# A two-layer pre-norm decoder on one core: norm statistics, causal maxima, rounding and residual biases moved between the engines, with new lists of the order of work

## The chip, the cores and the metric

The kernel runs on one core of a Trainium2 chip. A core has five engines with an instruction queue each, worked off in order: TensorE (PE; its weight loads are shown as PEld), VectorE (DVE), ScalarE (ACT), GpSimd (POOL) and SyncE (SP), which here only issues DMAs. They wait for one another by semaphores. Sums of products land in PSUM, everything else is in SBUF. The metric is the device time of one execution in microseconds (us); lower is better.

## What is computed

The input is 64 sequences of 128 tokens with 256 features, a context of the same shape and a mask. Six residual blocks follow one another, each on the layer norm of x, all in float32:

```python
x = x + L0_attn(layernorm(x))      # window attention: 7 neighbours, 16 heads; + bo
x = x + L0_xattn(layernorm(x))     # masked cross-attention to ctx; (.. @ Wp.T + bp) * mask
x = x + L0_ffn(layernorm(x))       # routing to 64 slots, a GRU step, back; + bo
x = x + L1_attn(layernorm(x))      # causal attention with a learned bias by position; + bproj
x = x + L1_xattn(layernorm(x))     # cross-attention to ctx; + bo
x = x + L1_ffn(layernorm(x))       # quantised linear, depthwise conv, silu, quantised linear

def layernorm(x):  m = mean(x, -1);  return (x - m) / sqrt(mean((x - m)**2, -1) + 1e-5)
# causal attention: att = softmax(q k / 4 + bias[h, t, s]), bias = -inf for s > t
# quantised linear: q = clip(round(x * s), -128, 127) / s, s = 127 / max|x| over the row
```

## The kernel before

Work comes in pieces of two sequences (B = 2). Four chains (0 to 3) take 8 turns each; a turn is all six blocks for one piece, so 32 pieces in all. A chain owns two PSUM banks, a tile `xa` (the residual stream, 128 tokens x 2 x 256), a tile `xn` (normalised x, reused in between) and an arena. The blocks are tagged a, b, f, 1, x, g in the order above.

Each engine's program of a turn is a Python generator (`vector_turn`, `scalar_turn`, `tensor_turn`, `pool_turn`, `sync_turn`), and each `yield` ends a step. `ORDER` holds for every engine a string of digits, one per step: the chain whose next step the engine's queue gets (`in_order`). So the interleaving of the chains on each engine is fixed in advance by these lists, and an engine that comes to a step whose operands are not there stands still, with everything behind it. From the third turn the strings repeat with every turn of the four chains; this text calls one repetition a round. All events of a chain are counted on one semaphore per engine, in the order that `TABLES` lists.

The parts that the change touches:

- A norm (`norm_vector`, L674 to L679): DVE takes statistics of each sequence (two `bn_stats`, two `bn_aggr`), adds 1e-5. GpSimd (`norm_pool`, L1515 to L1519) negates the mean, raises the variance to the power -0.5, multiplies both. ACT (L968) writes `xn = xa * rs + nm` for each sequence, and PE transposes it (L1170).
- Causal maxima (`maxima_vector`, L692 and L696): for each of 8 groups of four heads, DVE adds `pos_bias` to the scores in PSUM and writes them to SBUF (128x512), then reduces them to the negated maxima. ACT (L1034) takes `exp(s + m)`, one instruction per head, and PE transposes the result (L1286). The other two attentions call the same function with the reduction alone.
- Residual biases: bo, bproj and box are split into three bfloat16 parts in setup (L441 to L457); in each of the three blocks PE adds them by one product `pick` x `bias3` (L1319) in front of the projection (L1322). The addition to `xa` is one DVE instruction (L717, L792, L854), called y here.
- Rounding in g: DVE multiplies the hidden values by a scale (L904), ACT adds 12582912 (L1156), DVE subtracts it and casts to bfloat16 (L908).

Of the kernel before, what the change touches and what calls it, by code (L numbers as in the profile page):

```python
# [38 lines left out]
class Events:  # L39
# [10 lines left out]
    def now(self, name):  # L50
# [14 lines left out]
        wd_zero ones no_bias rel pos_max wd0 wd1 wd2 wd3 c2 bvw0 bvw1 bw10 bw11 bwx0 bwx1 slots c4 c5 c6 w1t_abs
        w1t_mean w1t_rec w1t_round w1t_min w1t c8 c9 c10 c_cw pos_eps pos_rec rel_norm c11 w2t_abs w2t_mean w2t_rec
        w2t_round w2t_min w2t c13 c14 c15 conn_d slot_mean slotT fire_b0 fire_b1 fire_b2 fire_b3 gate_b half_hn wvo
        bvo bias1 biasx bias_r0 bias_p0 bias_s0 bias_r1 bias_p1 bias_s1 bias_r2 bias_p2 bias_m0 bias_m1 bias_m2
# [4 lines left out]
        b_ve b_mx0 b_mx1 b_mx2 b_mx3 b_mx4 b_mx5 b_mx6 b_mx7 b_rc b_rm b_o b_y f_st0 f_st1 f_mv0 f_mv1 f_ve f_l
        f_top0 f_top1 f_sub f_mr0 f_mr1 f_m f_em f_s f_r f_al f_w1 f_w2 f_ac f_rz f_n1 f_n2 f_n3 f_u1 f_u2 f_u3 f_sv
        f_y 1_st0 1_st1 1_mv0 1_mv1 1_ve 1_bi0 1_mx0 1_bi1 1_mx1 1_bi2 1_mx2 1_bi3 1_mx3 1_bi4 1_mx4 1_bi5 1_mx5
        1_bi6 1_mx6 1_bi7 1_mx7 1_rc 1_o 1_y x_st0 x_st1 x_mv0 x_mv1 x_ve x_mx0 x_mx1 x_mx2 x_mx3 x_mx4 x_mx5 x_mx6
        x_mx7 x_rc x_o x_y g_st0 g_st1 g_mv0 g_mv1 g_ve g_am g_cl g_rc g_bk g_sc g_q2 g_hp0 g_hp1 g_t00 g_t01 g_t20
# [1728 lines left out]
```

## Time and profile before

| | |
|---|---|
| three runs | 3289.53, 3285.29, 3288.36 us; median 3288.36 |
| the profiled execution | 3283.83 us, its span 3282.0 us, mean granted clock 0.955 |
| PE, busy | 2836.4 us, 86% of the span |
| DVE, busy | 2522.0 us, 77% |
| ACT, busy | 2178.7 us, 66% |
| POOL, busy | 755.3 us, 23% |
| chain that ended last | PE 49%, DVE 31%, ACT 11%, POOL 4%, issue 4%, DMA 1% |

The spread of the three runs is 4 us. A busy share is an average over the whole span; which engine the others wait for changes inside a round, so the stretches have to be looked at apart. Instructions of one engine overlap a little: the busy time of a group is less than its count times the mean duration of one.

### The profile page before, as it was taken

The numbers are of one execution on the slowest core, as the hardware profiler recorded it, in microseconds if no ns is written. First come the engines' busy times: TensorE is split into PE (matmuls) and PEld (weight loads), VectorE is DVE, ScalarE is ACT, GpSimd is POOL, SyncE is SP. The second block draws the span as 40 slices with busy tenths as digits, with TensorE's granted clock in tenths as the row PEclk, the third lists the DMA queues.
The fourth block names the chain that finished last, engine by engine and source line by source line (L and its number), as shares of the span: only waits on it lengthen the run. The fifth ranks groups of instructions, "written<-read, shape, count | busy, mean of one in ns | idle before, by whom it ended". The sixth has DMA issues, their size and how long they took to land.

```text
span 3282.0 us, 59801 instructions
## 1 busy us (share of the span) xinstructions
PE 2836.4 (86%) x23406; PEld 2073.9 (63%) x23406; DVE 2522.0 (77%) x5446; ACT 2178.7 (66%) x4271; POOL 755.3 (23%) x1360
## 2 busy tenths in 40 slices
PE   3799986999878998899988998889988999889985
PEld 3566754676656766577666676567665676656763
DVE  6856599766898579975898769986799768987676
ACT  2368764678646876577855777657865687557773
POOL 1420013300233112330133112422032301232100
PEclk8799997999989999899999999999999999999996
DMA  5000010000000000000000000000000000000000
GB/s 157 1 1 1 4 27 17 1 1 5 24 12 9 1 16 12 20 1 1 16 21 11 1 4 13 24 9 1 5 24 12 9 1 16 16 17 1 1 1 13
DMA packets 43468, 43.47 MB, mean 13 GB/s; under 512 B 8577, under 2 KB 41185, under 8 KB 43185
## 3 DMA queue, kind: packets, MB, share of 16 engines
q1 hardware_dynamic: 41200, 36.46, 3.8%
q8 instruction: 184, 3.01, 0.4%
q10 hardware_dynamic: 1984, 3.18, 0.3%
q14 instruction: 100, 0.81, 0.1%
HBM read 31.24 MB, written 8.39 MB: 12 GB/s over the span
## 4 chain that ended last, share of the span: by engine, by line
PE 49%; DVE 31%; ACT 11%; POOL 4%; issue 4%; DMA 1%; SPq 0%; DVEq 0%; POOLq 0%; ACTq 0%
PE banks L1179 8%; PE banks L1213 7%; DVE chain_m L696 5%; PE banks L1322 4%; PE banks L1222 4%; PE banks L1260 4%; PE banks L1197 3%; DVE chain_arena L890 3%; PE banks L1286 2%; DVE chain_arena L927 2%; PE banks L1406 2%; DVE chain_arena L730 2%; DVE chain_arena L931 2%; DVE chain_stat L674 2%; DVE chain_arena L774 2%
## 5 line engine op out<-in xcount | busy, mean ns | idle before, releaser
L1213 PE MATMUL banks<-chain_arena 64*128 64x256 f32 x3072 | 426.2, 399 | 42.4 <-DVE chain_m L696 28.1
L696 DVE TENSOR_REDUCE chain_m<-banks 128x4 f32<-128x512 f32 x512 | 328.7, 681 | 84.8 <-PE banks L1213 84.2
L1515 POOL TENSOR_SCALAR chain_ng<-chain_sv 128x2 f32<-128x2 f32 x192 | 52.9, 276 | 1408.4 <-DVE chain_sv L677 1408.3
L1213 PEld LDWEIGHTS banks<-chain_arena 64*128 64x128 f32 x3072 | 286.0, 191 | 119.9 <-DVE chain_m L696 41.2
L1034 ACT ACTIVATE chain_arena<-chain_arena,chain_m 128x128 f32<-128x128 f32 x1024 | 324.1, 393 | 25.9 <-DVE chain_m L696 23.2
L968 ACT ACTIVATE chain_xn<-chain_xa,chain_nm,chain_rs 128x256 f32<-128x256 f32 x384 | 209.4, 596 | 166.3 <-POOL chain_nm L1519 165.5
L1260 PE MATMUL banks<-chain_arena 64*128 64x256 f32 x2048 | 268.2, 382 | 0.0
L692 DVE TENSOR_TENSOR chain_arena<-banks,pos_bias 128x512 f32<-128x512 f32 x256 | 174.9, 683 | 95.6 <-PE banks L1213 94.6
L1222 PE MATMUL banks<-chain_arena,chain_va 128*32 128x128 f32 x5120 | 198.1, 281 | 40.5 <-ACT chain_arena L1013 27.4
L1260 PEld LDWEIGHTS banks<-chain_arena 64*128 64x128 f32 x2048 | 200.5, 192 | 23.5
L1569 POOL TENSOR_TENSOR chain_arena<-chain_arena 128x512 f32<-128x512 f32 x128 | 169.5, 1341 | 148.4 <-DVE chain_arena L774 148.0
L1222 PEld LDWEIGHTS banks<-chain_arena,chain_va 128*32 128x32 f32 x5120 | 128.4, 111 | 106.5 <-ACT chain_arena L1013 45.8
L1179 PE MATMUL banks<-chain_arena,wqkv0T 128*128 128x256 f32 x768 | 187.2, 390 | 6.3 <-ACT chain_arena L975 6.3
L1013 ACT ACTIVATE chain_arena<-banks,chain_mask_k 128x1024 f32<-128x1024 f32 x128 | 142.4, 1114 | 73.3 <-PE banks L1260 73.0
L717 DVE TENSOR_TENSOR chain_xa<-banks,chain_xa 128x512 f32<-128x512 f32 x96 | 65.9, 686 | 157.3 <-PE banks L1322 157.1
L696 DVE TENSOR_REDUCE chain_m<-chain_arena 128x4 f32<-128x512 f32 x256 | 175.6, 686 | 8.8
L1286 PE MATMUL banks<-ident,chain_arena 128*128 128x128 f32 x1024 | 158.4, 281 | 18.2 <-ACT chain_arena L1034 17.5
L1013 ACT ACTIVATE chain_arena<-banks 128x1024 f32<-128x1024 f32 x128 | 131.6, 1028 | 61.8 <-PE banks L1260 61.5
L1179 PEld LDWEIGHTS banks<-chain_arena,wqkv0T 128*128 128x128 f32 x768 | 142.1, 193 | 34.0 <-issue 8.6
L774 DVE TENSOR_TENSOR chain_arena<-banks,chain_arena 128x512 f32<-128x512 f32 x224 | 146.4, 682 | 20.7 <-PE banks L1371 16.3
L1145 ACT ACTIVATE chain_arena<-chain_arena,pack 128x256 f32<-128x256 f32 x256 | 138.5, 595 | 32.5 <-DVE chain_arena L881 31.7
L1286 PEld LDWEIGHTS banks<-ident,chain_arena 128*128 128x128 f32 x1024 | 116.0, 141 | 68.3 <-ACT chain_arena L1034 29.8
(314 smaller groups left out, 6979.1 us busy)
## 6 DMA issues: line engine op xcount, KB each, us to landing
chain_xn<-in_ctx SPq DMA_DIRECT2D x32, 256.0 KB, 2.8
chain_xa<-in_x SPq DMA_DIRECT2D x32, 256.0 KB, 3.1
out<-chain_xa SPq DMA_DIRECT2D x32, 256.0 KB, 2.2
chain_arena<-in_mask SPq DMA_DIRECT2D x32, 128.0 KB, 3.5
f_w1t<-in_w1t ACTq DMA_DIRECT2D x1, 1024.0 KB, 7.0
f_w2t<-in_w2t ACTq DMA_DIRECT2D x1, 1024.0 KB, 14.3
wqkv0T<-in_wqkv0T ACTq DMA_DIRECT2D x1, 768.0 KB, 16.8
whh<-in_whh SPq DMA_DIRECT2D x1, 768.0 KB, 10.3
```

The costliest lines, as they stand in the source:

```text
L692: e.tensor_tensor(flat(t["s"][:, u % 4]), c.ps[:, u % 2, :], flat(k["pos_bias"][:, r]), ALU.add).then_inc(*done(f"{tag}_bi{u}"))
L696: e.tensor_reduce(m, s.rearrange("p (j o) t -> p j o t", o=2), AX.X, ALU.max, negate=True).then_inc(*done(f"{tag}_mx{u}"))
L774: e.tensor_tensor(halves(ring[:, slot]), bank(c, w % 2), halves(t["vp"])[:, :, w:w + T], ALU.mult).then_inc(*done(f"a_pv{w}"))
L968: e.activation(t["xn"][:, b, :], t["xa"][:, b, :], ACT.Identity, scale=t["rs"][:, b:b + 1], bias=t["nm"][:, b:b + 1]).then_inc(*done(f"{ta ...
L1013: e.activation(flat(t["p"][:, u % 2]), flat(ps), ACT.Exp, bias=t["mask_k"][:, b:b + 1] if masked else 0.0).then_inc(*done(f"{tag}_ex{u}"))
L1034: ex = e.activation(s, s, ACT.Exp, bias=max_of(t["m"], u // GROUPS, row_group(u), a))
L1179: mm = e.matmul(c.ps[:, i, N * m:N * m + N], w[:, j, c0 + 128 * m:c0 + 128 * m + 128], flat(src[:, j]), start=(j == 0), stop=(j == KT - 1))
L1213: mm[i] = e.matmul(c.ps[:, i, 2 * T * j:2 * T * j + 2 * T], t["qh"][p, j, x, b, :], flat(t["kx"][p, j, b]), start=not masked, stop=not mas ...
L1222: mm = e.matmul(out[32 * a:32 * a + 32, :], c.t["va"][:, b, VH * h:VH * h + 32], p(a), start=True, stop=True)
L1260: mm = e.matmul(ps[:, i, 2 * T * j:2 * T * j + 2 * T], t["kx"][p, j, b, o, :], t["qh"][p, j, :, b, :], start=False, stop=j == KT - 1)
L1286: mm = e.transpose(ps[:, u % 2, T * a:T * a + T], t["s"][:, u % 4, a, :], k["ident"][:])
L1569: e.tensor_tensor(flat(ring[:, slot]), flat(ring[:, slot]), flat(ring[:, slot + 1]), ALU.add).then_inc(*done(f"a_ac{w}"))
```

## The change

Five edits, and lists made anew for them:

1. Norms b, f, 1, x and g take their statistics elsewhere. The addition y to `xa` becomes two custom DVE instructions `tensor_tensor_reduce` (one per sequence), which also leave the row sum in `sm`. ACT turns it into the negated mean (`ng`), then squares `xa - mean` with the sum accumulated into `sq` (two instructions per norm). GpSimd divides by 256 and adds 1e-5, then goes on as before. Norm a stays as it was.
2. Causal maxima: four `tensor_tensor_reduce` (add, min, scale -1, one per head, 128x128) take the place of the addition and the reduction over 128x512. They leave `-(scores + bias)` in SBUF, so ACT's exp gets scale -1.
3. The three products on PE are gone. GpSimd adds the bias to `xa` (128x512, float32) after ACT has read `xa` for the norm; y waits for it. The split in setup is gone with them.
4. Rounding in g: DVE adds and subtracts 12582912 in one instruction; ACT's two are gone.
5. All five lists are new. A round is 368 steps of PE's list before and now. The four chains begin their turns at steps 0, 56, 98 and 143 of it before (chains 3, 0, 1, 2), and at 0, 59, 116 and 163 now (chains 1, 3, 2, 0).

```diff
+def add_rows(e, c, tag, rows):
+    for b in range(B):
+        x = c.t["xa"][:, b, :]
+        y = e.tensor_tensor_reduce(x, rows(b), x, 1.0, 0.0, ALU.add, ALU.add, c.t["sm"][:, b:b + 1])
+    y.then_inc(*c.dve.now(f"{tag}_y"))
...
         if bias:
-            e.tensor_tensor(flat(t["s"][:, u % 4]), c.ps[:, u % 2, :], flat(k["pos_bias"][:, r]), ALU.add).then_inc(*done(f"{tag}_bi{u}"))
-            e.wait_ge(*dve(f"{tag}_bi{u}"))
+            for a in range(PER):
+                mx = e.tensor_tensor_reduce(t["s"][:, u % 4, a], bank(c, u % 2)[:, a], k["pos_bias"][:, r, a // 2, a % 2], -1.0, 3e38, ALU.add, ALU.min,
+                                            max_of(t["m"], b, r, a))
+            mx.then_inc(*done(f"{tag}_mx{u}"))
...
-    e.tensor_tensor(flat(t["xa"][:]), c.ps[:, 1, :], flat(t["xa"][:]), ALU.add).then_inc(*done(f"{tag}_y"))
+    e.wait_ge(*pool(f"{tag}_xb"))
+    add_rows(e, c, tag, lambda b: c.ps[:, 1, D * b:D * b + D])
...
-        e.wait_ge(*act(f"g_ro{b}"))
-        e.tensor_scalar(t["hq"][:, :, b, :], cv[:, :, b, :], -ROUND, None, ALU.add).then_inc(*done(f"g_r2{b}"))
+        e.wait_ge(*dve(f"g_mu{b}"))
+        e.tensor_scalar(t["hq"][:, :, b, :], cv[:, :, b, :], ROUND, -ROUND, ALU.add, ALU.add).then_inc(*done(f"g_r2{b}"))
...
+def norm_scalar(e, c, n, tag, before=None):
+    if before:
+        e.wait_ge(*dve(f"{before}_y"))
+        e.activation(t["ng"][:], t["sm"][:], ACT.Copy, scale=-1.0 / D).then_inc(*done(f"{tag}_ng"))
+        e.wait_ge(*act(f"{tag}_ng"))
+        for b in range(B):
+            sq = e.activation(t["xn"][:, b, :], t["xa"][:, b, :], ACT.Square, bias=t["ng"][:, b:b + 1], accum_out=t["sq"][:, b:b + 1])
+        sq.then_inc(*done(f"{tag}_sq"))
+        yield
...
-    if bias is not None:
-        e.matmul(c.ps[:, 1, :], k["pick"][:, bias, :], spread(k["bias3"][:], 1, B), start=True, stop=False)
...
+    else:
+        e.wait_ge(*act(f"{tag}_sq"))
+        e.tensor_scalar(t["rv"][:], t["sq"][:], 1.0 / D, LN_EPS, ALU.mult, ALU.add).then_inc(*done(f"{tag}_ve"))
...
+def bias_pool(e, c, n, tag, k, i):
+    e.wait_ge(*c.act.of(n)(f"{tag}_xn{B - 1}"))
+    e.tensor_tensor(c.t["xa"][:], c.t["xa"][:], spread(k["res_bias"][:, i, :], 1, B), ALU.add).then_inc(*c.pool.now(f"{tag}_xb"))
...
     "vector": (
-        "3012333333000300031110222131133221332023313030021300320112201012021331121023232103321332000000112200"
+        "1320111111333133312223000121210021103112133133023130223323002211220231120011000011332033333322002222"
```

What stands in the queues now, at three places of a round in the repeated part. First DVE at a chain's y after an attention. Before, for chain 0 (`sums` and `xn` belong to the outputs in front of y; `stat`, `sv`, `rv` are the norm's; the rows behind are chain 2's routing):

```order
L705 RECIPROCAL chain0_sums<-banks 128x32
L711 TENSOR_TENSOR chain0_xn<-banks,chain0_sums 128x512
L717 TENSOR_TENSOR chain0_xa<-banks,chain0_xa 128x512
L674 BN_STATS chain0_stat<-chain0_xa 128x6 x2
L677 BN_AGGR chain0_sv<-chain0_stat 128x2 x2
L679 TENSOR_SCALAR chain0_rv<-chain0_sv 128x2
L801 TENSOR_TENSOR chain2_arena<-banks,b2f_r 128x128
```

Now, for chain 2 (`sm` is the row sum; the rows without an operand on the right read the accumulator out; the first three rows and the last are other chains'):

```order
L761 TENSOR_TENSOR chain1_arena<-banks,chain1_arena 128x512
L772 TENSOR_TENSOR chain1_arena<-chain1_arena 128x512
L776 TENSOR_TENSOR chain1_arena<-chain1_arena 128x512
L651 ISA chain2_xa,chain2_sm<-banks,chain2_xa 128x256
L651 ISA chain2_sm 128x1
L651 ISA chain2_xa,chain2_sm<-banks,chain2_xa 128x256
L651 ISA chain2_sm 128x1
L901 SCALAR_TENSOR_TENSOR chain3_xa<-banks,chain3_qs,chain3_xa 128x256
```

The norm's rows behind y are gone, y is four rows, and each `tensor_tensor_reduce` is two.

ACT at norms of block b in the same part of a round. Before (chain 1's and chain 0's norm, with other chains' copies and convolutions around them):

```order
L1133 COPY chain2_arena<-banks 128x512
L968 ACTIVATE chain1_xn<-chain1_xa,chain1_nm,chain1_rs 128x256 x2
L1023 COPY chain3_arena<-banks 128x512
L1145 ACTIVATE chain2_arena<-chain2_arena,pack 128x256 x4
L975 COPY chain1_arena<-banks 128x512
L1140 ACTIVATE chain2_arena<-chain2_arena 128x512
L968 ACTIVATE chain0_xn<-chain0_xa,chain0_nm,chain0_rs 128x256 x2
L1057 COPY chain1_arena<-banks 128x512
```

Now (`ng` and `sq` are the new first halves of a norm; the second half, with `nm` and `rs`, comes some rows later):

```order
L953 ACTIVATE chain0_xn,chain0_sq<-chain0_xa,chain0_ng 128x256 x2
L960 ACTIVATE chain3_xn<-chain3_xa,chain3_nm,chain3_rs 128x256 x2
L1036 COPY chain1_arena<-banks 128x2x128
L950 ACTIVATE chain2_ng<-chain2_sm 128x2
L953 ACTIVATE chain2_xn,chain2_sq<-chain2_xa,chain2_ng 128x256 x2
L967 COPY chain3_arena<-banks 128x512
L960 ACTIVATE chain0_xn<-chain0_xa,chain0_nm,chain0_rs 128x256 x2
L960 ACTIVATE chain2_xn<-chain2_xa,chain2_nm,chain2_rs 128x256 x2
L976 ACTIVATE chain3_arena<-banks,bq1,pack 128x256 x4
```

A norm takes two places in ACT's queue where it took one, and what stands in between belongs to other chains.

PE between the causal scores of a chain and the transposes of their exponentials. Before (chain 0; `arena` of chain 0 first as scores, last as exponentials):

```order
L1213 MATMUL banks<-chain0_arena 128x256 x4
L1396 MATMUL banks<-chain1_arena,chain1_xn 128x64 x4
L1398 MATMUL banks<-ones,chain1_arena 128x1
L1399 MATMUL banks<-ident,chain1_arena 128x128
L1170 MATMUL banks<-ident,chain3_xn 128x128 x4
L1406 MATMUL banks<-wihT,chain1_arena 128x512 x2
L1245 MATMUL banks<-ident_bf,chain2_m3 128x128 x8
L1411 MATMUL banks<-wihT,chain1_arena 128x256 x2
L1179 MATMUL banks<-chain3_arena,wqkvxT 128x256 x4
L1286 MATMUL banks<-ident,chain0_arena 128x128 x4
```

Now (chain 3, the same pair of steps):

```order
L1200 MATMUL banks<-chain3_arena 128x256 x4
L1390 MATMUL banks<-wihT,chain2_arena 128x512 x2
L1395 MATMUL banks<-wihT,chain2_arena 128x256 x2
L1232 MATMUL banks<-ident_bf,chain0_m3 128x128 x8
L1273 MATMUL banks<-ident,chain3_arena 128x128 x4
```

There were six steps of other chains between the two, and now there are three.

## Rows read from the trace of the kernel before

**Rows 1.** Windows: length; busy us (count) of PE, PEld, DVE, ACT, POOL; clock; DMA.

```profile
1608.00:1762.40 154.40, 129.29 (x1066) 93.16 (x1065) 143.97 (x297) 95.75 (x173) 48.83 (x80) 0.96 0.06 19
1762.40:1994.00 231.60, 216.56 (x1848) 160.43 (x1848) 163.57 (x372) 173.26 (x360) 45.28 (x89) 0.99 0.02 5
sum 386.00, PE 345.85 PEld 253.59 DVE 307.54 ACT 269.01 POOL 94.10; mean PE 172.92 PEld 126.79 DVE 153.77 ACT 134.51 POOL 47.05
```

**Rows 2.** Timeline of SP: start, length; chain 0's x loads of two turns.

```profile
1610.21 0.38 SPq L1610 DMA_DIRECT2D chain_xa<-in_x  x1
...
1996.57 0.38 SPq L1610 DMA_DIRECT2D chain_xa<-in_x  x1
```

**Rows 3.** Groups, 1608 to 1762.4: shapes, count | busy us, mean ns | idle before.

```profile
L717 DVE TENSOR_TENSOR chain_xa<-banks,chain_xa 128x512 f32<-128x512 f32 x4 | 2.7, 685 | 1.7 <-PE banks L1322 1.7
...
L692 DVE TENSOR_TENSOR chain_arena<-banks,pos_bias 128x512 f32<-128x512 f32 x4 | 2.7, 684 | 1.3 <-PE banks L1213 1.3
...
L1319 PE MATMUL banks<-bias,pick 128*128 128x512 bf16 x5 | 2.2, 431 | 0.6 <-DVE chain_arena L789 0.5
...
L792 DVE TENSOR_TENSOR chain_xa<-banks,chain_xa 128x512 f32<-128x512 f32 x2 | 1.4, 688 | 0.6 <-PE banks L1322 0.6
```

**Rows 4.** Groups, one round, 1608 to 1994.

```profile
L696 DVE TENSOR_REDUCE chain_m<-chain_arena 128x4 f32<-128x512 f32 x32 | 22.0, 686 | 1.1
...
L692 DVE TENSOR_TENSOR chain_arena<-banks,pos_bias 128x512 f32<-128x512 f32 x32 | 21.9, 683 | 8.3 <-PE banks L1213 8.2
...
L674 DVE BATCH_NORM_STATS2 chain_stat<-chain_xa 128x6 f32<-128x256 f32 x48 | 17.9, 415 | 1.7 <-DMA chain_xa<-in_x 1.3
...
L1156 ACT ACTIVATE chain_arena<-chain_arena,rounder 128x1024 f32<-128x1024 f32 x8 | 9.0, 1149 | 4.6 <-DVE chain_arena L904 4.6
...
L677 DVE BATCH_NORM_AGGREGATE chain_sv<-chain_stat 128x2 f32<-128x6 f32 x48 | 7.2, 173 | 0.0
...
L679 DVE TENSOR_SCALAR chain_rv<-chain_sv 128x2 f32<-128x2 f32 x24 | 5.0, 209 | 0.8
```

**Rows 5.** Groups, whole span: DVE additions from PSUM.

```profile
L851 DVE TENSOR_TENSOR chain_arena<-banks,bvo 128x256 f32<-128x256 f32 x32 | 13.4, 418 | 5.4 <-PE banks L1421 5.3
...
L801 DVE TENSOR_TENSOR chain_arena<-banks,b2f_r 128x128 f32<-128x128 f32 x32 | 9.1, 285 | 8.3 <-PE banks L1388 7.6
```

**Rows 6.** Timeline of DVE: small instructions in a row.

```profile
1702.03 0.21 DVE L898 TENSOR_SCALAR chain_qs<-chain_qs,w2t_back 128x2 f32<-128x2 f32 x1
1702.15 0.17 DVE L900 TENSOR_SCALAR chain_qs<-chain_qs 128x2 f32<-128x2 f32 x1
1702.22 0.38 DVE L738 TENSOR_REDUCE chain_arena<-banks 128x32 f32<-128x224 f32 x1
```

**Rows 7.** Groups, whole span: ACT on 128x256.

```profile
L968 ACT ACTIVATE chain_xn<-chain_xa,chain_nm,chain_rs 128x256 f32<-128x256 f32 x384 | 209.4, 596 | 166.3 <-POOL chain_nm L1519 165.5
...
L1105 ACT ACTIVATE chain_arena<-chain_arena 128x256 f32<-128x256 f32 x32 | 13.3, 416 | 6.0 <-DVE chain_arena L841 6.0
```

**Rows 8.** Timeline of PE: a bias product and its successor.

```profile
1791.67 0.38 PE L1319 MATMUL banks<-bias,pick 128*128 128x512 bf16 x1
1791.88 1.46 PE L1322 MATMUL banks<-wo0T,chain_arena 128*128 128x256 f32 x6
```

**Rows 9.** Timelines of DVE, POOL and ACT: one norm after cross-attention.

```profile
1712.56 0.69 DVE L717 TENSOR_TENSOR chain_xa<-banks,chain_xa 128x512 f32<-128x512 f32 x1
...
1714.35 0.23 POOL L1515 TENSOR_SCALAR chain_ng<-chain_sv 128x2 f32<-128x2 f32 x1 [11.41 <-DVE chain_sv L677]
...
1715.57 1.09 ACT L968 ACTIVATE chain_xn<-chain_xa,chain_nm,chain_rs 128x256 f32<-128x256 f32 x2 [0.38 <-POOL chain_nm L1519]
```

**Rows 10.** Waits, one round: total us, times, longest.

```profile
PEld banks L1170 <- ACT chain_xn L968: 8.7, 17, 3.4
```

**Rows 11.** Timeline of DVE: end of setup.

```profile
61.35 0.43 DVE L441 TENSOR_TENSOR bias_rows<-bias_rows,banks 32x256 f32<-32x256 f32 x1 [0.34 <-PE banks L563]
...
66.52 0.16 DVE L461 RECIPROCAL inv_tau<-tau 128x1 f32<-128x1 f32 x1
```

More of the change, by code:

```diff
@@ L64 @@
+        g_ve g_rs g_nm g_pad""".split(),
     "setup_dve": """
[L65 to L68, printed above, removed]
@@ L69 @@
-        bias3 tau inv_tau""".split(),
+        wd_zero ones rel pos_max wd0 wd1 wd2 wd3 c2 bvw0 bvw1 bw10 bw11 bwx0 bwx1 slots c4 c5 c6 w1t_abs w1t_mean
+        w1t_rec w1t_round w1t_min w1t c8 c9 c10 c_cw pos_eps pos_rec rel_norm c11 w2t_abs w2t_mean w2t_rec w2t_round
+        w2t_min w2t c13 c14 c15 conn_d slot_mean slotT fire_b0 fire_b1 fire_b2 fire_b3 gate_b half_hn wvo bvo tau
+        inv_tau""".split(),
     "dve": """
         a_st0 a_st1 a_mv0 a_mv1 a_ve a_qk0 a_qk1 a_qk2 a_qk4 a_qk5 a_qk6 a_mx a_sub a_sum a_cn a_sumc a_den a_rec
-        a_fw a_f1 a_r1 a_f2 a_f3 a_pv0 a_pv1 a_pv2 a_pv3 a_pv4 a_pv5 a_pv6 a_ac6 a_oT a_y b_st0 b_st1 b_mv0 b_mv1
@@ L73 @@
[L73 to L77, printed above, removed]
@@ L292, in setup_sync @@
         e.dma_start(k[name][:], tiles(inp[name])).then_inc(ld[name], 16)
[L293 to L294 removed]
+    for i, name in enumerate(("bo0", "bproj", "box")):
+        e.dma_start(k["res_bias"][:, i, :], rows(inp[name])).then_inc(ld["bias_rows"], 16)
     for name in ("bp", "b2f", "bof"):
@@ L342, in setup_vector @@
     e.wait_ge(*dve("ones"))
-    for i in range(GROUPS):
+    for i in range(2):
         e.tensor_scalar(k["pick"][:, i, :], k["ones"][:], k["rows_of"][:, i:i + 1], None, ALU.mult)
-    e.tensor_scalar(k["first"][:], k["ones"][:], k["rows_of"][:, GROUPS:GROUPS + 1], None, ALU.mult)
+    e.tensor_scalar(k["first"][:], k["ones"][:], k["rows_of"][:, 2:3], None, ALU.mult)
     e.wait_ge(ld["pack"], 16)
@@ L1075, in scalar_turn @@
     yield
-    yield from norm_scalar(e, c, n, "b")
+    yield from norm_scalar(e, c, n, "b", "a")
     e.wait_ge(*pe("b_T"))
@@ L1109, in scalar_turn @@
     yield
-    yield from norm_scalar(e, c, n, "1")
+    yield from norm_scalar(e, c, n, "1", "f")
     yield from normalized_scalar(e, c, n, "1", t["xnT"], 0)
@@ L1121, in scalar_turn @@
     yield from outputs_scalar(e, c, n, "x")
-    yield from norm_scalar(e, c, n, "g")
+    yield from norm_scalar(e, c, n, "g", "x")
     e.wait_ge(*dve("g_sc"))
@@ L1152, in scalar_turn @@
     yield
-    for b in range(B):
-        v = t["cv"][:, :, b, :]
-        e.wait_ge(*dve(f"g_mu{b}"))
-        e.activation(v, v, ACT.Identity, bias=k["rounder"][:, 0:1]).then_inc(*done(f"g_ro{b}"))
-        yield
 def flipped_tensor(e, c, n, tag, k, i):
@@ L1559, in pool_turn @@
     yield from norm_pool(e, c, n, "a", k)
+    yield from bias_pool(e, c, n, "a", k, 0)
     ring = t["ring"]
@@ L1582, in pool_turn @@
     yield from norm_pool(e, c, n, "1", k)
+    yield from bias_pool(e, c, n, "1", k, 1)
     yield from norm_pool(e, c, n, "x", k)
+    yield from bias_pool(e, c, n, "x", k, 2)
     yield from split_pool(e, c, n, "x")
```

298 lines of the change are left out of this document (137 added, 161 removed).

## Prediction

> **What bounds the kernel now.** I read the start times of chain 0's loads of x first, because they give the length of a round: 1996.57 - 1610.21 = 386.4 us [rows 2]. I use 386; the span of 3282 us is then 8.5 rounds, start and end included. The busy time by stretches of one round comes next [rows 1]. In the whole round PE is busy 345.9 of 386 us (90%), DVE 307.5 (80%), ACT 269.0 (70%), POOL 94.1. Cut in two it looks different. In the first 154.4 us (stretch A) DVE is busy 144.0, which is 93%, while PE has 129.3 (84%) and ACT 95.8 (62%): there the others wait for DVE. In the other 231.6 us (stretch B) PE is busy 216.6 (94%), DVE 163.6 (71%), ACT 173.3 (75%): there PE is the bound. So of PE's 40 idle us per round 25 lie in A. An edit that takes work off DVE is worth its full size in A only, and one that takes work off PE in B only.
>
> **The prices.** A causal group costs DVE 0.683 + 0.686 = 1.37 us, and a round has 32 [rows 4]. A norm costs 17.9 x 5/6 + 7.2 x 5/6 + 5.0 x 5/6 = 25.1 us per round over the 20 norms that change (4 of 24 are norm a), so 1.26 us each [rows 4]. A y costs 0.69 [rows 3]; there are 20 per round.
>
> The trace of before shows no `tensor_tensor_reduce`, so it is bounded. Its main instruction does what an addition from PSUM does: 0.285 us for 128x128, 0.418 for 128x256 [rows 5]. The accumulator read behind it is one more small instruction. It adds nothing if it hides wholly. A small instruction takes 0.17 us from start to end, and that is the other end. In a row of them the starts lie 0.12 and 0.07 us apart (1702.03, 1702.15, 1702.22) [rows 6], and I take about their middle, 0.085. So a pair of 128x128 costs 0.37 (0.285 to 0.455) and one of 128x256 0.50 (0.418 to 0.588).
>
> The Trainium skill speaks against such a split: VectorE: DVE Perf Modes, section "The TRN2 errata", says that each instruction pays its fixed cost and that tiles should have 512 elements or more; its table gives (120 + N) cycles at 0.96 GHz from PSUM. By that estimate four of 128 take 1.03 us, where the rows give 4 x 0.285 = 1.14 [rows 5]; the rows decide, and against two passes over 512 the split is still no loss.
>
> **DVE, whole round.** Removed: norms 25.1, y 20 x 0.69 = 13.7, causal 21.9 + 22.0 = 43.9, in all 82.7. Added: 40 pairs x 0.50 + 128 pairs x 0.37 = 67.4. Net -15.3 (-29.5 with the cheap pairs, -1.0 with the dear ones). DVE would go to about 292.
>
> **DVE in stretch A.** A has 6 y (4 and 2), so 6 of the changed norms, and 4 causal groups [rows 3]; their prices are the round's. Removed: 6 x 1.26 + 6 x 0.69 + 4 x 1.37 = 17.2. Added: 12 x 0.50 + 16 x 0.37 = 11.9. Net -5.3 us (-7.6 to -2.8). DVE is the bound here, so I count it in full. In B the rest of the relief meets an engine with 68 us to spare and is worth nothing.
>
> **PE.** 12 products per round. One lasts 0.38 us in the record, but its successor starts 0.21 us behind it (1791.67, 1791.88) [rows 8], and 0.21 is what its absence gives. Five of them lie in A [rows 3], where PE is not late; for B I count 7 x 0.21 = -1.5 us.
>
> **Rounding.** ACT loses 9.0 us per round [rows 4]; DVE's instruction keeps its shape. It sits in block g, where the hop over ACT is at the end of a turn: 1.15 us and two hand-overs less for each of four chains, of which other chains' steps cover most. I take -1.0 us (0 to -4).
>
> **ACT.** A square of 128x256 with one operand per partition lies between 0.416 (none) and 0.596 (two) [rows 7]; I take 0.50. Two in a row take 0.1 less than their sum (L968: 1.09 against 2 x 0.596) [rows 7, 9]: 0.90. With the small copy, 0.2 (0.1 to 0.416), a norm adds 1.1 us. Per round 22.0 - 9.0 = +13.0: ACT goes to 282, 73%. In A it is 6 x 1.1 = 6.6, against 3.6 removed if the roundings were spread evenly, so +3 on an engine at 62%; in B +10, to 183 of 231 us (79%). Nothing there is bound by it on average, and its cover is the work of other chains.
>
> **The path through a norm.** From the start of y to the start of the normalising pass it is 1715.57 - 1712.56 = 3.01 us now [rows 9]. Then: y 1.0, mean 0.2 and a hand-over 0.05, squares 0.9 and 0.05, POOL's scaling 0.23 (as L1515), power, product and the hand-overs as they are (1715.57 - 1714.58 = 0.99), in all 3.4 to 3.5: half a microsecond longer. This is not free: PE's weight loads of the transposes L1170 wait for that pass 17 times in a round of 24 norms, 8.7 us in all [rows 10], so of the 20 changed norms some 14 are late already. If all of these showed 0.5 us more, it would be 7 us. The lists leave as many steps between producer and transpose as before (I counted 7.3 on average both times), but DVE's queue in front of y is shorter. I take +2.5 us (0 to 7). POOL's 12 additions of about 1.3 us per round (15 of some 290 idle us) wait for nothing late; y comes several PE steps after the norm that frees `xa`. They cost nothing unless one stands in front of another chain's power.
>
> **Setup.** All engines wait for its last DVE instruction. From 61.35 + 0.43 on, until 66.52, stands the split of the biases [rows 11]; without it the two small ones for tau follow at once: -4.5 us.
>
> **The sum.** Per round -5.3 - 1.5 - 1.0 + 2.5 = -5.3; times 8.5 is -45; with setup -50. The profiled execution took 3283.83 us (span 3282.0) and would come to 3234. The median of the runs is 4.5 us above it, so the time compared is 3288 - 50 = 3238 us. With the ends of the terms this case runs from 3195 to 3268.
>
> **Rivals.**
> Better: the lists use the relief of B too. They are made anew, and the chains start a little more evenly apart (163 steps for the last one in place of 143), which would spread A's work of DVE over more of PE's. If PE came to 93% of a round, near its 94% in B now, the round would be (345.9 - 2.6) / 0.93 = 369 us, 17 less: 3288 - 144 - 4 = 3140. For it: DVE, ACT and PE would be closer together than now. Against: the sum of the three stays the same, and ACT's queue gets fuller. Chance 0.24.
>
> No change: the pair is dear. The Trainium skill, VectorE: DVE Perf Modes, section "The DRAIN you can't avoid", lets no DVE instruction start before the pipe of the one in front is empty, and its section "Two Vector instructions with no wait between them" makes the accumulator output a second instruction. As a mechanism of this kernel: 0.285 + 0.17 = 0.455 a pair, so A gives -2.8 only, and a causal group takes 1.82 us where it took 1.37. With 0.5 us more in front of each of 16 pairs of exponentials half covered, the round comes to -2.8 - 1.5 - 1.0 + 2.5 + 3 = 0: about 3284. The starts 0.07 and 0.12 us apart speak against it [rows 6]. Chance 0.09.
>
> Slower by the norm's path: each norm now enters ACT's queue twice and stands there behind other chains' work of up to a microsecond. If 0.5 us of that comes on top of the 0.5 for all 14 late norms, the term is 14 and not 2.5: -5.3 - 1.5 - 1.0 + 14 = +6.2 a round, +53 - 4 = 3337. It decides from a term of 7.8 on, 0.55 us at each late norm. For it: PE waits at these transposes now. Chance 0.12.
>
> Slower by a dear custom instruction, beyond the bounds of the nearest rows, say 0.6 us a pair. A: 12 x 0.73 + 16 x 0.6 = 18.4 against 17.2, +1.2. PE's lists now leave 3.25 steps of other chains between causal scores and transposes where they left 4.25 to 5.25; a step is 345.9 / 368 = 0.94 us, so 3.1 us of cover. The first group needs 2.4 + 1.35 (four exps) = 3.75, so 0.65 us shows 16 times a round: 10.4. Sum +1.2 - 1.5 - 1.0 + 2.5 + 10.4 = +11.6, +98 - 4 = 3382. It decides from about 0.49 us a pair. Against: nothing in the work differs from an addition. Chance 0.05.
>
> **How the numbers follow.** Forecast 0.50, better 0.24, no change 0.09, slower 0.12 + 0.05. A difference under 0.2% (6.6 us) can't be told from no change. The no-change case spreads evenly over the three. Faster 0.50 + 0.24 + 0.03 = 0.77, same 0.05, slower 0.18 (rounded). The range runs from 3130, just under the better case, to 3310: about 0.08 lie below, 0.12 above.
>
> **What would show it.** A `tensor_tensor_reduce` of 128x128 with its read, start to start: 0.37 us; 0.46 and more is the rival. DVE at 292 us a round, ACT at 282, PE at 343. The round at 381; 369 is the better case. The idle time of PE and its weight loads in front of the transposes of xn: 8.7 us a round [rows 10] grown to 11; grown by 8 or more, the norm's path. The setup ending 4.5 us earlier. The forecast is wrong if the stretch where DVE is over 90% busy keeps its length, or if DVE's relief comes with PE's share unchanged in both stretches.

## The result, and the profile after

The changed kernel takes 3314.05 us (median of 4 runs, 3311.59 to 3315.56), the kernel before 3288.95 beside it: 1.0076 times as long, 95% interval 1.0059 to 1.0094. The forecast was 3238 and faster.

The page of the kernel after, with the engines' busy time and the first line of the chain that ended last:

```profile
span 3309.8 us, 61738 instructions
PE 2830.2 (86%) x23310; PEld 2061.9 (62%) x23310; DVE 2247.9 (68%) x6647; ACT 2289.2 (69%) x5007; POOL 847.8 (26%) x1456
PE 43%; DVE 24%; ACT 19%; issue 5%; POOL 4%; DMA 3%; SPq 1%; DVEq 0%; POOLq 0%; ACTq 0%
```

DVE lost 274 us of work, ACT gained 110. Below are the loads of x that answer to [rows 2], and the window of that round, which answers to the sum of [rows 1]. By SP's list these loads are chain 1's here, and those of [rows 2] are chain 3's and not chain 0's; each is the chain that begins the round, and the length of a round is the same by either.

```profile
1602.43 0.38 SPq L1609 DMA_DIRECT2D chain_xa<-in_x  x1
...
1997.49 0.38 SPq L1609 DMA_DIRECT2D chain_xa<-in_x  x1
```

```profile
1602.40:1997.40 395.00, 345.99 (x2902) 253.39 (x2901) 273.94 (x820) 283.73 (x626) 104.32 (x180) 0.97 0.04 11
```

The round is 395.1 us, not 386.4, with the same 346 of PE: its idle time went from 40 to 49. Over four rounds (this chain's fifth last load of x to its last, divided by four) it is 393.7 against 385.65. The span's 28 us come from 15 saved up to the first of these five loads, 32 lost in the four rounds and 11 lost behind them.

Who PE waited for in one round: total us, times, longest. First the kernel before, rows that answer to [rows 10]:

```profile
PE banks L1213 <- DVE chain_m L696: 4.2, 6, 2.0
PE banks L1170 <- ACT chain_xn L968: 3.6, 3, 3.0
PE banks L1222 <- ACT chain_arena L1013: 3.4, 7, 1.1
PE banks L1286 <- ACT chain_arena L1034: 1.5, 2, 1.2
...
PEld banks L1213 <- DVE chain_m L696: 6.1, 8, 2.2
PEld banks L1222 <- ACT chain_arena L1013: 5.5, 8, 1.4
PEld banks L1286 <- ACT chain_arena L1034: 2.9, 4, 1.4
```

The kernel after (L1273 is L1286 of before, L1209 is L1222, L1157 is L1170, L1200 is L1213):

```profile
PE banks L1209 <- ACT chain_arena L1005: 7.1, 8, 1.2
PE banks L1273 <- ACT chain_arena L1026: 6.4, 5, 2.8
PE banks L1157 <- ACT chain_xn L960: 5.2, 5, 2.6
...
PEld banks L1273 <- ACT chain_arena L1026: 9.8, 12, 3.2
PEld banks L1157 <- ACT chain_xn L960: 9.6, 15, 2.8
PEld banks L1209 <- ACT chain_arena L1005: 9.4, 8, 1.5
...
PEld banks L1200 <- DVE chain_m L684: 0.4, 2, 0.2
```

I add up PE and its weight loads, whose waits overlap in part. For DVE's maxima they waited 10.3 us at L1213; at the same product after it is 0.4. ACT's exponentials stand in their place: 4.4 became 16.2 at the causal transposes (L1273), 8.9 became 16.5 at the heads' products (L1209). The norms grew from 12.3 to 14.8. PE changed the engine it waits for, and waits longer. That does not say yet that ACT became late; the section on the prediction looks at it.

### The profile page after: what moved, and what is told of

It is laid out like the page before. It is cut to its first block, busy times and chain, and to the rows that moved or that the text cites. A ratio compares the mean times of both kernels' runs of the same rounds, so it can differ in the third digit from the quotient of the medians.

```text
span 3309.8 us, 61738 instructions
## 1 busy us (share of the span) xinstructions
PE 2830.2 (86%) x23310; PEld 2061.9 (62%) x23310; DVE 2247.9 (68%) x6647; ACT 2289.2 (69%) x5007; POOL 847.8 (26%) x1456
## 4 chain that ended last, share of the span: by engine, by line
PE 43%; DVE 24%; ACT 19%; issue 5%; POOL 4%; DMA 3%; SPq 1%; DVEq 0%; POOLq 0%; ACTq 0%
PE banks L1166 8%; PE banks L1200 7%; ACT chain_arena L1026 4%; PE banks L1247 4%; PE banks L1209 3%; PE banks L1307 3%; DVE chain_m L684 3%; DVE chain_arena L761 2%; PE banks L1273 2%; PE banks L1184 2%; DVE chain_arena L717 2%; ACT chain_xn L960 2%; ACT chain_xn L953 2%; DVE chain_arena L915 2%; DMA chain_arena<-in_mask 2%
## 5 line engine op out<-in xcount | busy, mean ns | idle before, releaser
L1200 PE MATMUL banks<-chain_arena 64*128 64x256 f32 x3072 | 423.8, 399 | 9.7 <-DVE chain_m L684 4.4
L677 DVE CUSTOM_DVE_ANT_0 chain_arena<-banks,pos_bias 128x128 f32<-128x128 f32 x1024 | 226.9, 286 | 177.9 <-PE banks L1200 177.6
L1504 POOL TENSOR_SCALAR chain_rv<-chain_sq 128x2 f32<-128x2 f32 x160 | 31.8, 199 | 1222.5 <-ACT chain_xn L953 1218.8
L1200 PEld LDWEIGHTS banks<-chain_arena 64*128 64x128 f32 x3072 | 286.2, 191 | 85.5 <-issue 36.6
L651 DVE CUSTOM_DVE_ANT_0 chain_xa<-banks,chain_xa 128x256 f32<-128x256 f32 x320 | 122.4, 420 | 187.3 <-PE banks L1307 177.4
L1566 POOL TENSOR_TENSOR chain_arena<-chain_arena 128x512 f32<-128x512 f32 x128 | 169.7, 1337 | 279.8 <-DVE chain_arena L761 279.1
L1209 PE MATMUL banks<-chain_arena,chain_va 128*32 128x128 f32 x5120 | 195.7, 281 | 51.9 <-ACT chain_arena L1005 44.9
L1209 PEld LDWEIGHTS banks<-chain_arena,chain_va 128*32 128x32 f32 x5120 | 129.1, 111 | 122.6 <-ACT chain_arena L1005 62.1
L1273 PE MATMUL banks<-ident,chain_arena 128*128 128x128 f32 x1024 | 161.6, 282 | 44.8 <-ACT chain_arena L1026 43.7
L1273 PEld LDWEIGHTS banks<-ident,chain_arena 128*128 128x128 f32 x1024 | 115.6, 142 | 91.3 <-ACT chain_arena L1026 67.0
L1166 PEld LDWEIGHTS banks<-chain_arena,wqkv0T 128*128 128x128 f32 x768 | 144.2, 194 | 40.4 <-ACT chain_arena L967 12.3
L1157 PE MATMUL banks<-ident,chain_xn 128*128 128x128 f32 x640 | 126.6, 311 | 43.3 <-ACT chain_xn L960 39.7
L953 ACT ACTIVATE chain_xn<-chain_xa,chain_ng 128x256 f32<-128x256 f32 x320 | 160.0, 500 | 5.2
```

Source lines behind the costliest of these rows:

```text
L677: mx = e.tensor_tensor_reduce(t["s"][:, u % 4, a], bank(c, u % 2)[:, a], k["pos_bias"][:, r, a // 2, a % 2], -1.0, 3e38, ALU.add, ALU.min, ...
L953: sq = e.activation(t["xn"][:, b, :], t["xa"][:, b, :], ACT.Square, bias=t["ng"][:, b:b + 1], accum_out=t["sq"][:, b:b + 1])
L1166: mm = e.matmul(c.ps[:, i, N * m:N * m + N], w[:, j, c0 + 128 * m:c0 + 128 * m + 128], flat(src[:, j]), start=(j == 0), stop=(j == KT - 1))
L1200: mm[i] = e.matmul(c.ps[:, i, 2 * T * j:2 * T * j + 2 * T], t["qh"][p, j, x, b, :], flat(t["kx"][p, j, b]), start=not masked, stop=not mas ...
L1209: mm = e.matmul(out[32 * a:32 * a + 32, :], c.t["va"][:, b, VH * h:VH * h + 32], p(a), start=True, stop=True)
L1273: mm = e.transpose(ps[:, u % 2, T * a:T * a + T], t["s"][:, u % 4, a, :], k["ident"][:])
```

## The experiments

Letters for the edits: M custom maxima, R one-step rounding, P biases on POOL, N reworked norms. Two theories at first: "norms" (ACT's squares and the extra hops cost more than all else gives) and "lists" (the edits are good, the new order loses it). Each time has its ratio to the kernel before on the same chip.

**e1, M alone, old lists.**

```
-            e.tensor_tensor(flat(t["s"][:, u % 4]), c.ps[:, u % 2, :], flat(k["pos_bias"][:, r]), ALU.add)
-        e.tensor_reduce(m, s..., AX.X, ALU.max, negate=True)
+            for a in range(PER):
+                mx = e.tensor_tensor_reduce(t["s"][:, u % 4, a], bank(c, u % 2)[:, a], k["pos_bias"][...], -1.0, 3e38, ALU.add, ALU.min, ...)
```

> The kernel before and its lists, with one edit: the causal maxima (and the exponentials' sign) by the custom instruction; everything else as before. The trace after shows a group at 0.85 to 0.90 us where before it was 1.37, so DVE loses about 16 us of a round (32 groups), all of it off PE's queue. Theory 'norms' (the reworked norms eat the gain): this edit alone is faster, 3255 to 3280. Theory 'lists' (the edits are good, the new lists lose it): the same, 3255 to 3280. Theory 'DVE did not matter' (its waits turn into waits for ACT at once): 3284 to 3292, no change.

Measured 3275.80, 0.9968 [0.9957, 0.9979]: 11 us. PE's list is the same in both kernels, so A and B of [rows 1] can be cut at the same products: those that start at 1608.2 and 1762.5 in the kernel before start at 1601.4 and 1758.4 in e1. The windows between them, and chain 3's x loads four turns apart:

```profile
1601.40:1758.40 157.00, 130.68 (x1065) 93.62 (x1064) 143.39 (x320) 95.52 (x172) 47.45 (x80) 0.95 0.06 19
1758.40:1988.10 229.70, 215.41 (x1848) 160.34 (x1848) 152.73 (x540) 172.72 (x360) 44.70 (x88) 0.99 0.02 5
```

```profile
1219.75 0.38 SPq L1612 DMA_DIRECT2D chain_xa<-in_x  x1
...
2761.27 0.38 SPq L1612 DMA_DIRECT2D chain_xa<-in_x  x1
```

DVE lost 11.4 us of this round, only 0.6 of them in A (143.97 to 143.39), and A did not get shorter: it takes 157.0 us where it took 154.4. Over five rounds cut at the same products, A has a mean of 155.6 us against 154.4 with 1.3 us less of DVE's work in it, and B 229.6 against 230.8 with 10.9 less. The mean of four rounds is 1541.52 / 4 = 385.4 against 385.65. So DVE's work did not set the round, though DVE is 91% busy in A. Of the 10 us that the profiled span lost, 5 lie ahead of the first of these loads, 4 behind the last and 1 between them. By its time e1 is where "norms" and "lists" had it; by the round, it is the case "DVE did not matter".

**e5, M and R, old lists.** The two ACT steps of the rounding are dropped:

```
-        e.activation(v, v, ACT.Identity, bias=k["rounder"][:, 0:1]).then_inc(*done(f"g_ro{b}"))
-        e.tensor_scalar(t["hq"][:, :, b, :], cv[:, :, b, :], -ROUND, None, ALU.add)
+        e.tensor_scalar(t["hq"][:, :, b, :], cv[:, :, b, :], ROUND, -ROUND, ALU.add, ALU.add)
```

> Custom maxima and one-step rounding in the lists of before (ACT's less its two rounding steps); biases still by products on PE. It parts the 19 us that lie between the custom maxima alone (3276) and all edits but the norms (3295). Theory 'bias steps': POOL's in-order queue, with a step of 1.3 us and its wait for ACT in front of small steps of other sequences, is what costs; then this run keeps the gain: 3262 to 3280. Theory 'rounding': the DVE step that now waits for nothing of ACT moves the MLP's end in DVE's queue and costs; then this run is at 3288 to 3300.

Measured 3276.12, 0.9973 [0.9964, 0.9982]: as e1, so R is worth nothing that these runs can tell, and theory "bias steps" is left.

**e2, M, R and P, old lists.** Each bias step of POOL stands at the first place behind the pass that frees `xa`:

```
-    e.matmul(c.ps[:, 1, :], k["pick"][:, bias, :], spread(k["bias3"][:], 1, B), start=True, stop=False)
+    e.tensor_tensor(c.t["xa"][:], c.t["xa"][:], spread(k["res_bias"][:, i, :], 1, B), ALU.add)
```

> All edits but the reworked norms, in the lists of before (less the two rounding steps on ACT, plus three bias steps of POOL behind the norms a, 1 and x): custom maxima, one-step rounding, biases on POOL with no product on PE, the sums at the end of a layer with no row sum. ACT then does less than before, DVE 16 us a round less, PE 1.5 less. Theory 'norms': faster than before by 20 to 50 us, 3240 to 3270. Theory 'lists': the same 3240 to 3270. If it is 3285 or more, the cause lies in one of these edits (POOL's bias steps first), and both fall.

Measured 3295.08, 1.0025 [1.0014, 1.0036]: so both theories fall for these edits, and with e5, P cost 0.52%, 17 us, although it shortens the setup. POOL's timeline and DVE's waits over the whole span in e2 show it:

```profile
1785.31 2.52 POOL L1501 TENSOR_TENSOR chain_xa<-chain_xa,res_bias 128x512 f32<-128x512 f32 x2 [1.26 <-ACT chain_xn L951]
1787.78 4.94 POOL L1552 TENSOR_TENSOR chain_arena<-chain_arena 128x512 f32<-128x512 f32 x4
```

```profile
DVE chain_arena L756 <- POOL chain_arena L1552: 21.3, 18, 2.9
```

Two bias steps, which wait for ACT, stand in front of another sequence's window sums (L1552), and DVE waits 21.3 us for these; in e5 it was 2.6.

**e3, all edits, old lists.** DVE's list less its norm steps, each squares' step at the first place behind its sum.

> The code after, whole, in the lists of before: PE's and SP's lists unchanged, DVE's less its five norm steps, ACT's less two rounding steps and with each squares' step put in at the first place behind the sum that it needs, POOL's with the bias steps. Theory 'lists': 3230 to 3280, faster than before. Theory 'norms': ACT's squares and the two more hops of a norm are what costs, whatever the lists, and lists that leave no room for them do worse still: 3310 to 3380.

Measured 3355.06, 1.0208 [1.0187, 1.0229]. "Lists" fell in this form; but the placement was mine, as in e2.

**e4, after with tiny squares.** Each square runs over one column and leaves out the sum, so the kernel leaves out the variance.

```
-    sq = e.activation(t["xn"][:, b, :], t["xa"][:, b, :], ACT.Square, bias=t["ng"][:, b:b + 1], accum_out=t["sq"][:, b:b + 1])
+    sq = e.activation(t["sq"][:, b:b + 1], t["xa"][:, b, 0:1], ACT.Square, bias=t["ng"][:, b:b + 1])
```

> The kernel after with one line changed: the ACT squares of a norm run over 1 column instead of 256 and without the accumulator output, so the variances are wrong and the rest is computed as before. That takes about 1.0 us from every reworked norm's path (two of 0.50 + 0.19 us become two short ones) and 20 us from ACT in a round. Theory 'norms': the round falls from 395 by 5 to 15 us, 3190 to 3275. Theory 'lists': little changes, 3300 to 3315.

Measured 3282.15, 0.9982 [0.9971, 0.9993]: 31 us less than after, between what the two theories had said. 11.5 us less of ACT (283.7 to 272.2 a round) shortened the round by 3 (four rounds, 390.7 against 393.7).

That left a third theory, "fit": a set of lists is cut for the instructions it was made with. Each edit shifts work at dozens of places by a microsecond, and what it is worth depends on the room there.

**e6, after's lists, norms of before** (the five DVE instructions follow the sum in its step; ACT's squares' step issues nothing).

```
+    yield from norm_vector(e, c, n, {"b": "f", "1": "x", "x": "g"}[tag], f"{tag}_y")
+    if tag != "a":
+        yield
```

> The kernel after in its own lists, but with the norms of before: the five DVE instructions of a norm follow the sum in the same step of DVE's list, the sum is a plain tensor_tensor again, and the squares' step of ACT's list issues nothing. No list is changed. Theory 'norms' (ACT's squares and the extra hops are the loss, in any list): faster than after by 20 us or more, 3250 to 3295. Theory 'fit' (each set of lists fits the instructions it was made for; the edits shift work by a few us at many places, and what counts is the room that the lists leave there): slower than after, since DVE now has 1.9 us more in front of other sequences' work at each of 20 places a round: 3325 to 3380.

Measured 3347.82, 1.0198 [1.0182, 1.0213]. "Norms" fell: what cost 1.83% in the old lists (e3 less e2) gains 1.22% in the new ones, as "fit" had it.

**e9, after's lists, biases on PE** (POOL's bias steps issue nothing: `-    yield from bias_pool(e, c, n, "1", k, 1)`, `+    yield`).

> The kernel after in its own lists, with the residual biases back as products on PE; the three bias steps of POOL's list issue nothing. PE gets its 12 products a round back (1.5 to 2.5 us), POOL loses 15.6 us a round. Theory 'bias steps' (POOL's steps of 1.3 us in front of small ones cost what they cost in the old lists, where they went with 19 us): faster than after by 12 us or more, 3285 to 3302. Theory 'fit' (after's lists were made with room for them): within 10 us of after, 3304 to 3324.

Measured 3309.97, 1.0066 [1.0051, 1.0081]: as after, within the intervals.

**e12, after's lists, maxima of before** (the diff of e1, reversed).

> The kernel after in its own lists, with the causal maxima in two DVE instructions as before (0.68 + 0.68 us a group instead of 0.85 for both). The same edit was worth 11 us in the lists of before. Theory 'fit' (the new lists are laid out for the short form; whatever is undone in them costs more than it was worth in the old ones): slower than after by 25 to 70 us, 3340 to 3385. Rival 'worth is a property of the edit': slower by 8 to 16 us, 3322 to 3330.

Measured 3361.79, 1.0218 [1.0201, 1.0235]: M is worth 1.42%, 47 us, in these lists, four times its 0.32% in the old ones.

**e7 and e8, other lists, no instruction changed.** About half the steps moved (1389 of ACT's 2688, by 0.8 place on average). A piece of ACT's list after and in e7 (chain, step; the fifth turn, and e7's list differs a little from turn to turn), around the first causal exponentials of chain 0:

```
after  0:ex0 2:sq 0:ex1 0:pc0 2:xn1 3:oc 0:pc1 2:xnT 0:ou0
e7     0:ex0 3:ou1 2:sq 0:ex1 2:xn1 3:oc 0:pc0 2:xnT 0:pc1
```

> The code after, not one instruction changed, in other lists: from its own lists, single steps of one sequence were moved by up to 12 places, in all turns alike or in one, and a move was kept where a replay with the durations of the traces did not get longer. Theory 'fit': the same instructions in other lists lose most of PE's 49 idle us a round, 3130 to 3250. Theory 'norms': the longer path of a norm is in every list, so no list brings it under the time before: 3290 to 3330.

> The code before, no instruction changed, in lists found from its own in the same way and with as many tries as those of e7. It says what the edits are worth once both codes have lists of like quality. Theory 'fit': 3140 to 3260, and above e7 by 5 to 40 us, so that the edits are a small gain by themselves. Theory 'norms': e8 is below e7 by 20 us or more.

Measured: e7 3211.61, 0.9779 [0.9765, 0.9794]; e8 3208.06, 0.9769 [0.9752, 0.9785]. That is 98 us off the code after and 76 off the code before. "Fit" had e8 5 to 40 us under e7, "norms" 20 or more; it is 3.5 under it, so neither had the pair right. In the piece shown the squares of another chain stand between the two exponentials in both; e7 only lets a norm's pass and a copy ahead of `pc0`. The waits of e7 that answer to those of after (L1272 is L1273 there):

```profile
PE banks L1208 <- ACT chain_arena L1004: 4.6, 5, 1.2
PE banks L1156 <- ACT chain_xn L959: 3.1, 2, 1.9
...
PE banks L1272 <- ACT chain_arena L1025: 0.8, 2, 0.4
...
PEld banks L1156 <- ACT chain_xn L959: 6.9, 13, 2.2
PEld banks L1208 <- ACT chain_arena L1004: 6.2, 6, 1.5
...
PEld banks L1272 <- ACT chain_arena L1025: 2.9, 9, 0.7
```

With the same squares on ACT, the 16.2 us at the causal transposes are 3.7, the 16.5 at the heads 10.8, the 14.8 at the norms 10.0. The round shown is 379.2 us (380.4 over four rounds) where it was 395.0. PE's idle time fell from 49 to 38 us, so most of it is still there, against what "fit" expected. The other 4.5 us are PE's busy time, 346.0 to 341.5, at a granted clock of 0.99 where it was 0.97.

**e10 and e11, parts of the change in lists found alike.**

```
e10: M, R           e11: M, R, N          (e8: none, e7: M, R, P, N)
```

> Custom maxima and one-step rounding only (the code of e5), in lists found as those of e7 and e8, with as many tries. With lists of like quality e8 (no edit) took 3208 and e7 (all edits) 3212. If these two edits are worth their 11 us in good lists too, and norms and biases give it back: 3185 to 3202. If the edits are worth nothing in any good lists: 3203 to 3215.

> All edits but the biases on POOL, in lists found in the same way. It parts the norms from the biases. If the biases on POOL are what gives the gain of the other edits back: 3185 to 3202, as e10. If the reworked norms are: 3205 to 3225, as e7 or more.

Measured: e10 3175.66, 0.9652 [0.9638, 0.9667], faster than either case had it; e11 3203.60, 0.9742 [0.9728, 0.9757], between the two.

The lists of these searches have two origins. Those of e8 and e10 (and of e13 and e15 below) were found from the lists of before, those of e7 and e11 (and e14 and e16) from those of after. A step of PE's list stands about one place from where it stood in its origin, and 71 places on average from where it stands in a list of the other origin.

**e13 to e16, the same four codes, lists of a second search** (other random moves, each code from the same start as in the first).

```
e13: none   e14: M, R, P, N   e15: M, R   e16: M, R, N
```

> The code before in lists of a second search, other random moves, as many tries. Gives the spread of a search. Theory 'edits' (differences between codes in searched lists belong to the edits): within 10 us of the first, 3198 to 3218. Rival 'luck of the search': off by 15 us or more.

> The code after in lists of a second search. Theory 'edits': 3202 to 3222, level with e13. Rival 'luck': off by 15 us or more from 3212.

> Custom maxima and one-step rounding only, lists of a second search. Theory 'edits': 3166 to 3186, 20 us or more under e13 and e16. Rival 'luck': 3190 to 3215, level with the others.

> All edits but the biases on POOL, lists of a second search. Theory 'edits' (the norms on ACT cost 20 to 30 us in good lists): 3194 to 3214, 20 us or more over e15. Rival 'luck': off by 15 us or more from 3204, or within 12 us of e15.

Measured: e13 3206.86, 0.9759 [0.9741, 0.9776]; e14 3204.69, 0.9750 [0.9734, 0.9765]; e15 3178.03, 0.9673 [0.9651, 0.9695]; e16 3202.40, 0.9745 [0.9729, 0.9761]. No code moved by more than 7 us (0.3% by the ratios), so differences of 24 us and more are not luck of the search. That they belong to the edits is shown only between codes whose lists have the same origin: for M and R, and for P. N and "all four" compare lists of two origins, and what the origin is worth is part of their last column. No run parts it. In per cent of the time before, from differences of the ratios:

| edit | old lists | new lists | searched lists, mean of two |
|---|---|---|---|
| M | -0.32 (e1) | -1.42 (e12) | |
| R | +0.05 (e5 less e1) | | |
| M and R | -0.27 | | -1.02 (e10, e15 less e8, e13) |
| P | +0.52 (e5, e2) | +0.10, not told from 0 (e9) | +0.21, not told from the spread of a search |
| N | +1.83 (e2, e3) | -1.22 (e6) | +0.81, with the origin (e11, e16 less e10, e15) |
| all four | +2.08 (e3) | +0.76 (after) | 0.00, with the origin (e7, e14 less e8, e13) |

The old lists' values of P and N hold my placement of the added steps. The 0.76% of the change itself is all four edits and the step from the old lists to the new.

The fastest version is e10: M and R only, 3175.66 us. Its page and a round, from x load to x load:

```profile
span 3168.0 us, 61273 instructions
PE 2794.4 (88%) x23406; PEld 2058.2 (65%) x23406; DVE 2424.6 (77%) x6982; ACT 2099.9 (66%) x4207; POOL 760.3 (24%) x1360
...
sum 370.60, PE 338.66 PEld 250.95 DVE 294.88 ACT 260.18 POOL 94.31; mean PE 338.66 PEld 250.95 DVE 294.88 ACT 260.18 POOL 94.31
```

PE's idle time is 32 us a round, from 40. The other 7 us of the round are PE's busy time, 338.7 from 345.9, at a granted clock of 0.99 (before: 0.96 in A and 0.99 in B).

## Why the prediction was wrong

**The step that failed is "DVE is the bound here, so I count it in full" in stretch A.** -5.3 of the -5.3 us of a round hung on it, since the other terms cancelled. The runs showed 0 in its place. e1 took 11.4 us of a round off DVE with no other change, and the mean round went from 385.65 to 385.4; A, with 0.6 to 1.3 us less of DVE's work, took 157.0 us where it had taken 154.4 (155.6 against 154.4 over five rounds). In the change itself DVE lost 33.6 us of a round (307.5 to 273.9), and the round got 8 us longer. A busy share of 93% said how full DVE was, not that PE waited for its throughput. What PE waits for is single hand-overs in a fixed order, the longest of them 3.2 us in the rows above. The Trainium skill, Perfetto Trace Analysis, section "Identifying the Most-Contended Engine", says to optimise the engine with the highest occupancy first; the page's section "Optimization Strategy" adds that this engine can change over time. In stretch A the runs do not bear the first out: DVE, the busiest engine there, was relieved and the stretch did not get shorter.

**The second is that the lists were taken as neutral** ("leave as many steps between producer and transpose as before"). e7 moved steps by about one place on average and took 98 us off the same instructions, so lists that look alike in such a count are not worth the same. In my own rival on the dear instruction I had noted that the new PE list leaves 3.25 steps in front of the causal transposes in place of 4.25 to 5.25, and had used it only there. With a cheap instruction 16.2 us of a round still wait there, for ACT.

Whether ACT had become late can be read from the traces. Each instruction has a place in the lists, so it can be given to its chain, turn and step. The table has means over the third to the seventh turn (80 cases, norms 100), in us from the end of the PE step in front. "ACT done" is when ACT has finished what the next PE step needs, "PE free" is when PE has worked off the other chains' steps in between, and "idle" is what PE's products then lose in a round (its weight loads not counted).

| ACT done, PE free, idle | before | after | e7 |
|---|---|---|---|
| first causal group (L1286) | 4.0, 5.4, 1.2 | 3.2, 3.6, 2.6 | 2.8, 4.1, 0.4 |
| second causal group (L1286) | 7.2, 8.3, 0.4 | 5.1, 5.8, 3.3 | 4.8, 5.9, 1.0 |
| heads' products (L1222) | 1.6, 2.0, 3.8 | 1.5, 2.0, 6.4 | 1.6, 2.1, 3.9 |
| transposes behind a reworked norm | 6.3, 7.5, 3.5 | 7.3, 8.9, 4.2 | 6.6, 8.3, 1.9 |

At the causal groups ACT is done earlier than before, and PE is back earlier still. By the lists 4.8 steps of other chains stood in front of the first group's transposes before, 3.5 stand there now and 3.9 in e7. So between ACT's end and PE's return there were 1.4 us, then 0.5, and 1.3 again in e7. At the heads' products the means did not move at all, only the idle time did; why, these means do not show. Only at the norms is ACT later, by 1.0 us, and there PE's list gave 1.4 us more room. So what changed at the causal transposes is PE's list, and not that ACT got later.

**The sum had two more flaws.** It multiplied a round's change by 8.5, start and end included, but the 8 us that a round got longer are 28 us of the span and not 68: the four rounds lost 32, the end 11, and the start won 15. And with all terms at their ends (-13.1 and +2.7 us a round) the case runs from 3172 to 3307 us, not from 3195 to 3268. The measured 3314 lies outside both.

Point by point:
- The pair: forecast 0.37 and 0.50 us, measured 0.21 and 0.34 from start to start, under the lower ends. The main instruction's 0.286 and 0.420 were as read from [rows 5], but the next one starts before it has ended:

```profile
1608.92 0.29 DVE L677 CUSTOM_DVE_ANT_0 chain_arena<-banks,pos_bias 128x128 f32<-128x128 f32 x1 [0.35 <-PE banks L1200]
1609.13 0.08 DVE L677 DVE_READ_ACCUMULATOR2_ANT chain_m<- 128x1 f32 x1
1609.13 0.29 DVE L677 CUSTOM_DVE_ANT_0 chain_arena<-banks,pos_bias 128x128 f32<-128x128 f32 x1
```

- DVE per round: forecast 292, measured 273.9, for the most part for the same reason. It bought nothing.
- ACT: forecast +13.0 to 282, measured +14.7 to 283.7. The square took 0.50 as taken. Missing was the accumulator's read, 0.19 us behind each, so two squares last 1.09 us and not 0.90.
- The norm's path, forecast 0.5 us longer. The norm behind cross-attention that answers to [rows 9]:

```profile
1705.98 0.40 DVE L651 CUSTOM_DVE_ANT_0 chain_xa<-banks,chain_xa 128x256 f32<-128x256 f32 x1
...
1707.16 0.21 ACT L950 ACTIVATE chain_ng<-chain_sm 128x2 f32<-128x2 f32 x1
1707.40 0.51 ACT L953 ACTIVATE chain_xn<-chain_xa,chain_ng 128x256 f32<-128x256 f32 x1
1707.81 0.19 ACT L953 ACTIVATION_READ_ACCUMULATOR chain_xn<-chain_xa,chain_ng 128x1 f32 x1
1707.90 0.49 ACT L953 ACTIVATE chain_xn<-chain_xa,chain_ng 128x256 f32<-128x256 f32 x1
...
1708.58 0.19 POOL L1504 TENSOR_SCALAR chain_rv<-chain_sq 128x2 f32<-128x2 f32 x1 [1.18 <-ACT chain_xn L953]
...
1709.89 1.09 ACT L960 ACTIVATE chain_xn<-chain_xa,chain_nm,chain_rs 128x256 f32<-128x256 f32 x2
```

  From sum to pass it is 3.91 us, 0.9 more than the 3.01. Over the 140 reworked norms of the second to the eighth turn, matched step by step in both traces, the mean went from 4.55 to 5.70. Yet the waits at the transposes grew by just the 2.5 us a round of the term (PE 3.6 to 5.2, PEld 8.7 to 9.6). The rival "slower by the norm's path" had the sign and about the size of the result, but not its place: the wait at the norms is its term of 2.5 and not 14. Whether the norms cost anything in good lists is open: the 0.81% of the searched lists is also the difference of two origins.
- PE, busy: forecast 343, measured 346.0. The 12 products are gone (2914 to 2902 matmuls), the busy time is not, and e9, which brought them back, was no slower.
- Rounding: -1.0 forecast, 0 measured (e5). POOL's additions "cost nothing unless one stands in front of another chain's power": so it was, with window sums in place of the power (e2).
- Setup: forecast 4.5 us, measured 66.52 to 61.22, 5.3.
- The better case expected lists that use B's relief. Such lists exist (e10), but the change did not bring them, and no code reached its 3140.

What stays open is at which places the room lies that makes M and R worth 1.0% in searched lists and 0.3% in the old ones; only the totals were measured. P and N were searched only on top of M and R. No code was searched from both origins, so what N and all four edits are worth in good lists is not known. How far e10's lists are from the best is not known.

## What to carry to other kernels

Where the order on every engine is fixed, an engine's busy share over a stretch does not say what relief of it is worth; one run with that work shortened does, and it costs one kernel. Compare two codes only in lists made with like effort and from the same start: the same edit was worth between -1.2% and +1.8% here, and moving steps by about one place was worth more (2.3 to 3.0%) than all four edits together. A shorter instruction gains only if the lists keep the work that stood in front of the engine that waits; here PE's new list came back to the causal transposes 1.7 us earlier and spent the gain. A step given to an engine has to be judged by what stands behind it in that engine's list, as the bias steps of e2 in front of POOL's window sums.
